# Causal masks moved from VectorE to TensorE, b1 issued ahead of the bias columns, GpSimd's clearing put later, W2 issued by ScalarE

## The reference

```
x = x + attn(layernorm(x))                # 16 heads of 8 channels, causal
  qkv  = x @ w_qkv + b_qkv
  attn = softmax(where(causal, q @ k.T / sqrt(8), -inf)) @ v
  out  = attn @ w_proj + b_proj
x = x + ffn(layernorm(x))                 # 8 experts, 128 -> 512 -> 128
  probs   = sigmoid(x @ Wg + bg);  weights = probs * (probs > 0.5)
  h       = relu(x @ W1[e] + b1[e])
  result  = sum over e of weights[:, e] * (h @ W2[e] + b2[e])
```

## Time and profile before

| | us |
|---|---|
| median of 3 executions | 678.09 |
| the profiled execution, its own time | 677.06 |
| its span, first to last instruction | 675.3 |
| TensorE matmul busy | 652.4 (97%) |
| VectorE busy | 450.6 (67%) |
| ScalarE busy | 443.2 (66%) |
| GpSimd busy | 339.1 (50%) |
| granted TensorE clock, mean | 0.977 |

### The profile page before, as it was taken

One profiled execution on the slowest core, in us unless ns is written; L12 is line 12 of the kernel. 1 busy time (PEld: TensorE's weight loads), 2 busy tenths in 40 slices (PEclk: granted clock), 3 DMA queues, 4 the chain that ended last, 5 costly groups with the idle time before them and its releaser, 6 DMA issues.

```text
span 675.3 us, 12981 instructions
## 1 busy us (share of the span) xinstructions
PE 652.4 (97%) x4325; PEld 439.9 (65%) x4325; DVE 450.6 (67%) x1019; ACT 443.2 (66%) x857; POOL 339.1 (50%) x445
## 2 busy tenths in 40 slices
PE   4989998999999999999999999999999999999998
PEld 3445565667666766667666766666666766677776
DVE  6757786678676876678676876678576776344343
ACT  2446768667766776667776786667666667646543
POOL 5117444457545654457545654456645554554453
PEclk7958999999999999999999999999999999999999
DMA  5441224220322122220322122221322010100200
GB/s 178 97 138 23 57 47 110 58 57 19 92 64 57 48 58 57 73 57 25 93 56 59 48 58 58 73 58 34 79 54 50 31 34 33 49 33 33 79 31 17
DMA packets 24560, 40.08 MB, mean 59 GB/s; under 512 B 3312, under 2 KB 12920, under 8 KB 24496
## 3 DMA queue, kind: packets, MB, share of 16 engines
q1 hardware_dynamic: 24112, 38.89, 20.8%
q10 hardware_dynamic: 384, 0.38, 0.2%
HBM read 23.46 MB, written 2.23 MB: 38 GB/s over the span
## 4 chain that ended last, share of the span: by engine, by line
PE 90%; DVE 3%; ACT 2%; issue 1%; DMA 1%; POOL 1%; SPq 0%; ACTq 0%; DVEq 0%; POOLq 0%
PE ring L1273 11%; PE y_bank L1398 10%; PE ring L1353 10%; PE ring L1206 9%; PE ring L1208 9%; PE ring L1207 9%; PE y_bank L1405 9%; PE y_bank L1400 9%; PE ring L1280 4%; PE ring L1212 3%; DVE f_buf L1174 1%; PE ring L1295 1%; ACT xn L870 1%; PE ring L1369 1%; PE y_bank L1273 1%
## 5 line engine op out<-in xcount | busy, mean ns | idle before, releaser
L969 ACT ACTIVATE h_hi<-ring 128x512 fp32r<-128x512 f32 x256 | 152.6, 599 | 110.4 <-PE ring L1208 106.7
L937 ACT ACTIVATE pt<-ring 128x512 f32<-128x512 f32 x312 | 171.0, 599 | 53.0 <-PE ring L1273 51.1
L845 POOL TENSOR_TENSOR h_lo<-h_all,h_hi 128x512 fp32r<-128x512 f32 x96 | 123.6, 1288 | 161.4 <-ACT h_all L975 143.1
L1161 DVE SCALAR_TENSOR_TENSOR h_lo<-ring,h_hi 128x512 fp32r<-128x512 f32 x160 | 109.1, 685 | 57.1 <-ACT h_hi L969 57.1
L838 POOL TENSOR_SCALAR_AFFINE_SELECT pt<-pt 128x512 f32<-128x512 f32 x128 | 79.8, 637 | 94.5 <-ACT pt L937 94.3
L1094 DVE CUSTOM_DVE_ANT_0 ring<-causal,ring 128x512 f32<-128x512 bf16 x124 | 83.3, 713 | 51.8 <-PE ring L1273 51.8
L1398 PE MATMUL y_bank<-h_hi,w_lo 128*128 128x512 f32 x256 | 110.8, 433 | 2.7 <-DVE f_buf L1174 2.7
L1206 PE MATMUL ring<-x2T_lo,w_hi 128*128 128x512 f32 x256 | 101.9, 398 | 0.0
L1273 PE MATMUL ring<-stack 32*128 32x384 f32 (+3 forms) x998 | 97.1, 372 | 4.9 <-DMA stack<-nmT 2.9
L1208 PE MATMUL ring<-x2T_hi,w_hi 128*128 128x512 f32 x256 | 101.2, 395 | 0.0
L1400 PE MATMUL y_bank<-h_hi,w_hi 128*128 128x512 f32 x256 | 101.2, 395 | 0.0
(11 more groups left out here) (145 smaller groups left out, 795.8 us busy)
## 6 DMA issues: line engine op xcount, KB each, us to landing
f_buf<-gates SPq DMA_DIRECT2D x32, 512.0 KB, 3.7
stack<-parts SPq DMA_DIRECT2D x95, 128.0 KB
x_in<-in_x SPq DMA_DIRECT2D x8, 256.0 KB, 3.0
f_buf<-in_W SPq DMA_DIRECT2D x2, 1024.0 KB, 7.7
out_x<-f_buf SPq DMA_DIRECT2D x7, 256.0 KB, 2.4
stack<-nmT SPq DMA_DIRECT2D x64, 8.0 KB
stack<-stack SPq DMA_DIRECT2D x28, 16.0 KB
out_x<-f_buf SPq DMA_DIRECT2D x2, 128.0 KB, 1.9
```

The lines of the kernel that those rows point to most:

```text
L845: g_.tensor_tensor(h_lo[:, (i * SLOTS + s) % H_RING, :], h_all[:], h_hi[:, (i * SLOTS + s) % H_RING, :].bitcast(F32), ALU.subtract).then_i ...
L937: sc.activation(pt[:, slot, :], b[:], ACT.Exp, scale=SCALE).then_inc(free_sem("ex", i, g, u), 1)
L969: sc.activation(h_hi[:, (i * SLOTS + s) % H_RING, :], bank_of("z", i, s)[:], ACT.Relu).then_inc(s_hhi, 1)
L1161: v.scalar_tensor_tensor(out=h_lo[:, (i * SLOTS + s) % H_RING, :], in0=bank_of("z", i, s)[:], scalar=0.0, in1=h_hi[:, (i * SLOTS + s) % H_ ...
```

## The change

- TensorE adds the mask for query block 3 too: one more product of line 1280's kind, 128 columns wide, for each of the 128 units; every max unit now ends with its mask. VectorE takes a plain maximum over all 512 columns in place of the combined instruction. The tile `causal` shrinks to the two 128-column masks.
- ScalarE's queue issues b1 (three times) before the bias columns.
- GpSimd's stackset, and vset behind it, wait for VectorE's blocks b1 and wqk.
- ScalarE issues the load of W2, not SP.
- The planner's costs of two transfers at the start (b1 600 to 1200, w1 2500 to 1900), the engine of w2load, the new wait, and the table SHIFT change; the lists of all engines come out anew.

```diff
--- before.py
+++ after.py
@@ -47,8 +47,7 @@
 LAST_TERM = (BATCH - 1, EXPERTS - 1)
 
 
-def masked_by_pe(unit):
-
+def rows_of_two_heads(unit):
 
     return MAX_UNITS[unit[-1]][0] != 3
 
@@ -87,35 +86,34 @@
 
 
 
-SHIFT = {('act', 'exp', False): 23.0,
-         ('act', 'exp', True): 3.5,
-         ('act', 'nm', False): 15.0,
-         ('act', 'nm', True): -2.5,
-         ('dve', 'klo', False): 4,
-         ('dve', 'merge', False): 8,
-         ('dve', 'merge', True): -2,
-         ('dve', 'qlo', False): 3.0,
-         ('dve', 'smax', False): -4.5,
+SHIFT = {('act', 'exp', False): 25.5,
+         ('act', 'nm', False): 25.0,
+         ('act', 'nm', True): -4.5,
+         ('dve', 'hlo', False): -3,
+         ('dve', 'merge', False): 2,
+         ('dve', 'merge', True): -2.0,
+         ('dve', 'smax', False): -5.0,
          ('dve', 'smax', True): -4,
-         ('dve', 'w1', False): 4.0,
-         ('dve', 'xT', False): 5.0,
-         ('dve', 'yT', True): 7.5,
+         ('dve', 'w1', False): 3.5,
+         ('dve', 'xT', False): 10.0,
          ('pe', 'ex', False): 3.0,
-         ('pe', 'ex', True): -11.5,
          ('pe', 'gate', False): -11.0,
          ('pe', 'k', False): 4.5,
-         ('pe', 'max', False): 12.5,
+         ('pe', 'max', False): 17.0,
+         ('pe', 'max', True): 3.0,
          ('pe', 'pv', False): 4.0,
          ('pe', 'q', False): 3.0,
+         ('pe', 'q', True): 6,
          ('pe', 'v', False): 4.5,
-         ('pe', 'w1', False): 0.5,
+         ('pe', 'w1', False): 6.0,
          ('pe', 'y', False): 1,
          ('pe', 'y', True): 1.0,
          ('pe', 'yT', False): 7,
          ('pe', 'yT', True): 1,
          ('pe', 'yU', False): 6,
          ('pe', 'ylo', False): -0.5,
-         ('pool', 'nm', False): 10.5}
+         ('pool', 'causal', False): -4,
+         ('pool', 'causal', True): 9.5}
 
 
 def work_items():
@@ -133,20 +131,20 @@
 
     put("dma", ("x0", None), -62, 4000)
     put("dma", ("wqkv", None), -61, 500, ("dma", ("x0", None)))
-    put("dma", ("b1", None), -60.5, 600, ("dma", ("wqkv", None)))
-    put("dma", ("w1", 0), -60, 2500, ("dma", ("b1", None)))
+    put("dma", ("b1", None), -60.5, 1200, ("dma", ("wqkv", None)))
+    put("dma", ("w1", 0), -60, 1900, ("dma", ("b1", None)))
     put("dma", ("w1", 1), -59, 3000, ("dma", ("w1", 0)))
     put("dma", ("small", None), -58.5, 2000, ("dma", ("w1", 1)))
     put("dma", ("x1", None), -58, 1000, ("dma", ("small", None)))
-    put("sp", ("w2load", None), -8.9, 600, ("pe", ("w1", EXPERTS - 1)))
-    put("dma", ("w2", None), -8, 9000, ("sp", ("w2load", None)))
+    put("act", ("w2load", None), -8.9, 700, ("pe", ("w1", EXPERTS - 1)))
+    put("dma", ("w2", None), -8, 9000, ("act", ("w2load", None)))
     put("pool", ("ident", None), -60, 700)
     put("pool", ("center", None), -60, 1400, ("pool", ("ident", None)))
     put("pool", ("mask", None), -59, 1300)
     put("dve", ("b1", None), -20.5, 2700, ("dma", ("b1", None)), ("dve", ("ln1b", 0)))
     put("dve", ("wqk", None), -19.9, 1300, ("dma", ("wqkv", None)), ("dve", ("b1", None)))
     put("dve", ("stackset", 0), -40, 1765)
-    put("pool", ("stackset", 1), -20, 2200, ("pool", ("rs1", 0)))
+    put("pool", ("stackset", 1), -20, 2200, ("pool", ("rs1", 0)), ("dve", ("wqk", None)))
     put("act", ("stack", 0), -17, 100, ("dve", ("klo", 0)), ("dve", ("qlo", 0)), ("pool", ("stackset", 1)))
     put("pool", ("vset", None), -10, 2400, ("pool", ("stackset", 1)))
     put("pe", ("small", None), 20, 1500, ("pool", ("center", None)), ("dma", ("small", None)))
@@ -364,7 +362,7 @@
         for unit in ex:
             at(now + cost + AFTER_PE, "done", ("pe", unit))
         for unit in mx:
-            if not masked_by_pe(unit):
+            if not rows_of_two_heads(unit):
                 at(now + cost + AFTER_PE, "done", ("pe", unit))
             else:
                 cost += MASK_COST + (ENTER["mask"] if form == "scores" else 0)
@@ -496,8 +494,8 @@
         ident = sb("ident", [P, P])
         ident16 = sb("ident16", [P, P], BF16)
         ident32 = sb("ident32", [P, P], F32R)
-        causal = sb("causal", [P, T + P], BF16)
-        mask16 = causal[:, T - P:].rearrange("p (n k) -> p n k", n=2)
+        causal = sb("causal", [P, 2 * P], BF16)
+        mask16 = causal[:].rearrange("p (n k) -> p n k", n=2)
         mhalf = sb("mhalf", [P, TB])
         wqkv_in = sb("wqkv_in", [P, 3 * C])
         wqk_hi = sb("wqk_hi", [P, 2, C], F32R)
@@ -696,10 +694,6 @@
                     if i:
                         sp.dma_start(rows[M_ROW::M_STEP, :, 0, :],
                                      rows[M_ROW + 4::M_STEP, :, 0, :]).then_inc(s_stack[g], 16)
-                elif kind == "w2load":
-                    sp.wait_ge(*full("w1", EXPERTS - 1))
-                    sp.dma_start(w2_in[:].rearrange("p a (c d) -> p (a c) d", d=C),
-                                 w2.rearrange("e (c p) d -> p (e c) d", p=P)).then_inc(s_w2, 16)
                 elif kind == "mrow":
                     g = w[2]
                     sp.wait_ge(*emptied("nm", i, g))
@@ -798,6 +792,8 @@
                                      bp[:].rearrange("p (a c) -> p a c", a=1)
                                      .broadcast_to([P, TB, C]), ALU.add).then_inc(s_xbp, 1)
                 elif kind == "stackset":
+                    pool.wait_ge(s_wset, 6)
+                    pool.wait_ge(s_b1, 5)
                     g_.memset(stack_half(1), 1.0).then_inc(s_stackset, 1)
                     g_.memset(nm[:].bitcast(F32), 0.0).then_inc(s_stackset, 1)
                 elif kind == "vset":
@@ -859,10 +855,10 @@
         def _(act):
             sc = nc.scalar
             act.dma_start(wqkv_in[:], w_qkv).then_inc(s_wqkv, 16)
-            act.dma_start(b_cols[:], b_cols_in).then_inc(s_bcols, 16)
             act.wait_ge(s_b1zero, 1)
             for k in range(3):
                 act.dma_start(b1_in[32 * k:32 * k + EXPERTS, :], b1).then_inc(s_b1load, 16)
+            act.dma_start(b_cols[:], b_cols_in).then_inc(s_bcols, 16)
 
             def normalise(n, i, src, dst, done):
                 act.wait_ge(s_rs[n], i + 1)
@@ -882,6 +878,10 @@
                     act.wait_ge(*full("w1", i))
                     b = bank_of("w1", i)
                     sc.activation(w1_hi[:, i * T:(i + 1) * T], b[:], ACT.Copy).then_inc(s_w1hi, 1)
+                elif kind == "w2load":
+                    act.wait_ge(*full("w1", EXPERTS - 1))
+                    act.dma_start(w2_in[:].rearrange("p a (c d) -> p (a c) d", d=C),
+                                 w2.rearrange("e (c p) d -> p (e c) d", p=P)).then_inc(s_w2, 16)
                 elif kind == "w2":
                     act.wait_ge(s_w2, 16)
                     sc.activation(w2_hi[:, i * T:(i + 1) * T], w2_in[:, i, :],
@@ -1089,17 +1089,12 @@
                     j = heads[0]
                     if u == 4:
                         wait(dve, s_merge, 2 * (i * GROUPS + g))
-                    if qb == 3:
-
-                        v.tensor_tensor_reduce(
-                            out=b[:], in0=causal[:, 0:T], in1=b[:], scale=-1.0, scalar=-MASKED,
-                            op0=ALU.add, op1=ALU.min,
-                            accum_out=negmax[:, g, qb, j % 2, j // 2:j // 2 + 1]
-                        ).then_inc(free_sem("max", i, g, u), 1)
-                        continue
                     if qb == 20:
                         dst = pm[:, j % 2, j // 2, :]
                         src = b[:].rearrange("p (n k) -> p n k", k=P)
+                    elif len(heads) == 1:
+                        dst = negmax[:, g, qb, j % 2, j // 2:j // 2 + 1]
+                        src = b[:]
                     else:
                         dst = negmax[:, g, qb, j % 2, :]
                         src = b[:].rearrange("p (n k) -> p n k", n=2)
@@ -1269,15 +1264,20 @@
                         if k >= len(pieces):
                             continue
                         out_, lhsT, rhs = pieces[k]
-                        stop = k == len(pieces) - 1 and not (kind == "max" and masked_by_pe(unit))
+                        stop = k == len(pieces) - 1 and kind == "ex"
                         last = mm(out_, lhsT, rhs, start=(k == 0), stop=stop, skip_group_check=True)
                         if stop:
                             last.then_inc(full_sem(kind, *unit), 1)
-                for unit in filter(masked_by_pe, mx):
+                for unit in mx:
                     blocks = bank_of("max", *unit)[:].rearrange("p (n k) -> p n k", k=P)
                     qb = MAX_UNITS[unit[2]][0]
-                    dst = blocks[:, 2:4, :] if qb == 20 else blocks[:, 1::2, :]
-                    mm(dst, ident16[:], mask16, start=False, stop=True,
+                    if qb == 3:
+                        dst, mask = blocks[:, 3, :], mask16[:, 0, :]
+                    elif qb == 20:
+                        dst, mask = blocks[:, 2:4, :], mask16
+                    else:
```

(2 more changed lines are left out.)

## The result

The changed kernel takes 681.99 us (median of 11 runs, 679.87 to 685.26) against 677.55 us of the kernel before beside it (11 runs, 677.03 to 679.82): ratio 1.006, interval 1.0044 to 1.0077. It is slower by 0.6%, or 4.4 us. I had forecast 674.8 us and a range up to 678.7.

The account below looks back on a forecast made before the run. TensorE was taken to bound the long middle, other engines and transfers the first 57 us. Start gain 6.2 us, masks 2.9 us: 677.06 - 6.2 + 2.9 = 673.8 profiled, 1.0 under the median, so 674.8 us; range 669.5 to 678.7.

Parts of the forecast that it names:

- Part A: Start-up: b1 issued earlier and its cast freed of GpSimd's clearing bring line 1061 and q forward 3.2 us (3.0 to 3.5).
- the floor of ScalarE's copy: Start-up: line 1061 can't start before ScalarE's second copy of x^T is done, at 11.63 us.
- nine tenths: Share of the start-up gain of 6.9 us let through to the end: 6.2 us.
- Part B: Start-up: W2 leaves SP's queue, so the first maxima row lands sooner; 3.5 us gained (1.45 to 5.2).
- with W2 on ScalarE's queue SP has nothing before this transfer: First maxima row's transfer: basis of the upper bound, 7.35 - 2.15 = 5.2 us gained.
- not under 4.5: Sign of being right: the first row of maxima lands within 4.5 us of its issue.
- not before 36.5: Sign of being right: the first exponential product comes before 36.5 us.
- Part D: Score loop: 128 more masks on TensorE cost 0.06 us in each of 49 visits, 2.9 us in all (0 to 5.9).
- the other 15 fall where TensorE waits or runs fillers, at nothing: Score loop: of 64 masked visits, the 15 outside the 49 counted after 110 us cost nothing.
- My upper bound of a visit: Score loop: two narrow masks can't cost more than two wide ones, 0.12 us a visit, 5.9 us for 49.
- The new due times: All engines' reordered lists: priced at nothing, with 1.5 us on either side.
- Rival (1): Score loop: weights, not columns, set a mask's pace; 49 visits take 5.9 us, 680.6 us in all; chance 0.12.

Follow-up runs that it names:

- s2: Kernel before, old lists, with only b1 ahead of the bias columns and GpSimd's late clearing; W2 stays on SP: 672.11 us, ratio 0.9913.
- m1: Kernel before, lists untouched, with only query block 3's masks moved to TensorE (128 columns) and plain maxima on VectorE: 683.70 us, ratio 1.0097.
- s3: Kernel before, lists kept but for W2's load, which ScalarE issues in place of SP: 676.87 us, ratio 0.9982.
- s1: Kernel before, old lists but for W2's load, with all start edits (b1 first, late clearing, W2 by ScalarE), no masks: 672.38 us, ratio 0.9927.
- w1: Kernel before, lists kept but for W2's load, which SP issues just behind the first maxima row: 674.75 us, ratio 0.9917.
- k1: Kernel before with all the change's edits but its old lists (W2's load alone moved): 679.25 us, ratio 1.0014.
- u1: Changed kernel with its new lists and start edits, query block 3 masked by VectorE's combined instruction again: 673.78 us, ratio 0.9947.
- m2: As m1, but the added masks are 256 columns wide: 687.97 us, ratio 1.0153.
- c1: Kernel before, lists kept, with b1 first, late clearing and W2 behind the first maxima row on SP, masks on VectorE: 670.43 us, ratio 0.9832.

## Why the prediction was wrong

**Part A's mechanism held, and its size was too low.** I took 3.2 us at line 1061 and 3.1 were measured, 3.65 at q. Line 1061 did not come down to the floor of ScalarE's copy (done at 11.37 us now); it starts at 12.05 right behind VectorE's own block. Alone, with the old lists (s2), part A gives 5.3 us at the end, where nine tenths of 3.2 are 2.9. The sum had left out the clock. TensorE from 11 to 27.5 us, before and in s2:

```profile
11.00:27.50 16.50, 12.31 (x40) 6.69 (x41) 11.12 (x31) 6.53 (x13) 2.35 (x7) 0.73 0.32 74
```
```profile
11.00:27.50 16.50, 14.95 (x66) 7.96 (x67) 13.78 (x37) 8.23 (x16) 5.61 (x9) 1.00 0.50 113
```

Before, TensorE idles longer ahead of these products and then runs q and k at half clock, 0.43 us from start to start; in s2 they are 0.23 apart. So line 1061 starts 2.6 us sooner (12.53 against 15.16), q's first product 4.1 us (13.22 against 17.28), the first scores 5.2 us (20.34 against 25.54). The size of this differs between executions with the clock; m1 and s3, with the old start, had 0.90 in that stretch.

**Part B failed,** the step "with W2 on ScalarE's queue SP has nothing before this transfer", taken at 3.5 us of a range of 1.45 to 5.2. It gave nothing in s1 against s2 (672.4 and 672.1 us) and 0.6 us between medians in s3, which can't be told from none. I bounded it from below by another small transfer under W1's traffic; the rows of the same transfer had the answer: it landed when W2 was nearly through (41.74 against 42.7 us), whatever its issue took. The measured landing was 7.29 us after the issue, not under 4.5, and the first exponential product came at 38.29 us, not before 36.5. By the Trainium skill (DMA: Bandwidth & Descriptors, Queues, rings and completion order) a transfer's semaphore write comes only after all earlier writes of that DMA engine, across its queues. The landings at the end of W2's traffic in three kernels agree with that rule, but the rule is not what held the transfer: its data itself did not move for the first 5 us (no packet on q1 above), and w1, with nothing ahead, lands in 2.3 us. Why its packets stay behind another queue's, no run here shows. That page's other rule, that issuing elsewhere saves the issuing time, would have given 2.8 us; here the issuing time was saved and the end was not moved.

**Part D failed in its size,** the largest miss of the sum. The masks took 6.6 us in the old lists and 8.2 in the new ones, not 2.9. The price of a visit in the middle was 0.076 where I took 0.06, so 3.7 to 3.9 us for 49. The step that failed is "the other 15 fall where TensorE waits or runs fillers, at nothing": they took 2.4 us by 103 us, more a visit than in the middle (0.16 against 0.076). Two reasons, both in m1's trace: a visit that had followed a visit now leaves the tiling and comes back (0.89 to 1.41 us above), and a filler in a fixed list gives no time back when real work is put ahead of it (the lateness stands unchanged over the fillers). I had read the fillers as slack and the dense 57 to 100 us as unpaced; the masks show that work added there stays late for good. My upper bound of a visit, 0.12 us from the wide masks of the middle, was taken from visits with full products as neighbours and did not hold for the others.

**The new due times,** priced at nothing with 1.5 us on either side, cost 2.7 us with the masks (changed against k1, whose intervals lie apart); without them (u1 against s1) it is 1.4 us, and there the intervals overlap. What in them does is open: the changed kernel has 110 fillers where the old lists have 84, and it computes the second sequence's k before the first value product and not after, but I ran no kernel that tells these apart. In its profiled execution the clock also fell for 3.4 us at 11.5 us, which k1's did not, and about 0.4 us of it may be ScalarE's late copy of the maxima, shown with the result.

**The sum in hindsight:** 677.5 - 4.7 (start) + 6.6 (masks) + 2.7 (lists) = 682.1, against 682.0 measured. That it comes out is no test, since the 2.7 is what was left over; the test of the rest is k1. Against the forecast of -6.2 + 2.9 the start gave 1.5 us less (part B's nothing, partly made good by a part A larger than priced, which was luck), the masks took 3.7 more and the lists 2.7 more. Neither of the last two makes a clear loss alone: k1, without the new lists, can't be told from the kernel before, and u1, without the masks, is faster than it. With the masks at my 2.9 the sum would be 678.4, just within the range. Rival (1) named the right side and the right mechanism, the masks, with the wrong reason for their price: m2 shows that columns count.

## What to carry to other kernels

Price an added TensorE product by its neighbours: ahead of a full product it cost under 0.04 us here, among fillers and row-tiled visits 0.06 to 0.1, and fillers in a fixed order are no slack for it. Before moving a large load to another queue, ask what lands while it is on its way: moving it behind the small transfer gained where moving it to another engine gained nothing that could be told. An engine that has room (VectorE, a third idle) was here the right place for work that the full one could take, even where its instruction looks clumsy.

## What the runs showed of the hardware that I had not expected

- A small transfer (two of 8 KB) issued while 2 MB were on their way landed 7.0 to 7.4 us after its issue in six kernels, with the 2 MB on its own queue or on another, 0.3 to 1.5 us before their own landing, and after 2.3 us with nothing ahead. In the changed kernel 747 packets of the other queue moved before its first.
- The granted clock of the start differs between executions of one kernel, and it outweighs the edits: c1 took 662.8 us at a mean of 1.000 and 673.0 at 0.977; w1 666.7 at 0.997 and 674.9 at 0.980. Taking 33 fillers away put the kernel before at 0.964 to 0.970 in all six executions and cost 3.7 us.
- A VectorE cast of 72x512 from SBUF to SBUF took 3.09 us beside GpSimd's clearing and ended with it, past the end of one clearing instruction (9.40 us) to that of the next (11.29); it takes 0.42 without. A subtraction with one PSUM input beside the same clearing kept its 0.63 us.
